# Last value tile of a masked attention read-out: its third piece sent as two transfers, rows 0 to 119 and rows 120 to 127

## The chip, the cores and the metric

One core of a Trainium2 chip runs the whole kernel. The metric is the device time of one execution in microseconds; smaller is better. Everything is float32.

## What is computed

For 512 users, each with 200 items of 64 numbers, the reference forms a query, scores the items, masks them, takes the softmax, and sums the projected values:

```python
B, L, D = (512, 200, 64)
scaler = jnp.float32(D) ** 0.5
q = target_key @ W_target.T
k = jnp.einsum('bld,ed->ble', item_keys, W_item)
v = jnp.einsum('bld,ed->ble', item_values, W_value)
scores = jnp.einsum('bd,bld->bl', q, k) / scaler
scores = scores + -100000000.0 * (1.0 - mask.astype(scores.dtype))
w = jax.nn.softmax(scores, axis=1)
return jnp.einsum('bl,bld->bd', w, v)
```

## The kernel before, in words

Keys and values are 26 MB each, and nearly all of the time is spent bringing them in. The kernel never projects keys or values: the query goes through both weight matrices first, and the value weights are applied once to the weighted sum.

The users go in four blocks (`NBLK`) of 128. Each block has two key tiles and two value tiles (`NT`), each of 128 rows by 6400 numbers, which is 3200 KB. `key_ring` and `value_ring` have two slots each, `s` = 0 and 1. SyncE (SP) issues all of these transfers from one queue, in the order key 0, key 1, value 0, value 1, and from the second block on it waits with each issue until TensorE (PE) has used up the slot (`s_key_used`, `s_value_used`).

A value tile has three regions along its row: 2 "eighth" column groups of 128 numbers, 16 "half" groups, and 32 "full" groups. TensorE works them off in `weigh(n, s)`: `weigh_full(s, k)` for k = 0 to 7 issues four matmuls each (L378), and `weigh_rest(s)` issues 2 for the eighths (L387) and 16 for the halves (L393). For slot 0 the full groups come first and the rest after; for slot 1 it is the other way round. All of them add up in `ps_context`. A float32 matmul stands in the trace as two records, so the 32 full matmuls of a tile are 64 records.

The very last value tile (block 3, slot 1) is not one transfer but four, cut along the row at `CUTS = (0, 5, 7, PAIRS_T)` (L162):

- piece 0: eighths and halves, 2304 numbers of each row, 1152 KB
- piece 1: the full groups of k = 0 to 4, 2560 numbers, 1280 KB
- piece 2: the full groups of k = 5 and 6, 1024 numbers, 512 KB
- piece 3: the full groups of k = 7, 512 numbers, 256 KB

Each has its own semaphore `s_value_piece[c]`, and TensorE waits for it before `weigh_rest`, before k = 0, before k = 5 and before k = 7. After the last matmul a short tail follows: VectorE copies the context (L306), TensorE transposes it (L422), VectorE masks it (L314), TensorE projects it (L430), ScalarE scales it (L233) and sends it out (L236).

Of the kernel before, what the change touches and what calls it, by code (L numbers as in the profile page):

```python
# [10 lines left out]
P = 128  # L11
# [21 lines left out]
def masked_attention_kernel(nc, w_query, targets, w_value_cols, mask_rows, keys, values, out):  # L33
# [13 lines left out]
    HALF_AT = EIGHTHS_T * VB  # L47
    FULL_AT = HALF_AT + N_HALF * VB
    CUTS = (0, 5, 7, PAIRS_T)

    out_blocks = out.rearrange("(n u) d -> n u d", u=P)

    with ExitStack() as ctx:
        def sb(name, shape, dt=F32):
            return ctx.enter_context(nc.sbuf_tensor(name, shape, dt))
# [4 lines left out]
        def sem(name):  # L60
            return ctx.enter_context(nc.semaphore(name))

        key_ring = sb("key_ring", [P, NT, KCOLS])
        value_ring = sb("value_ring", [P, NT, VCOLS])
# [46 lines left out]
        s_value = [sem(f"s_value{s}") for s in range(NT)]  # L111
        s_value_piece = [sem(f"s_value_piece{c}") for c in range(len(CUTS))]
        s_key_used = sem("s_key_used")
# [33 lines left out]
        @block.sync  # L147
        def _(sp):
            for n in range(NBLK):
                for s in range(NT):  # L150
                    if n > 0:
                        sp.wait_ge(s_key_used, NT * (n - 1) + s + 1)
                    sp.dma_start(key_ring[:, s, :], keys[n * NT + s]).then_inc(s_key[s], 16)
                for s in range(NT):
                    if n > 0:
                        sp.wait_ge(s_value_used, NT * (n - 1) + s + 1)
                    tile = values[n * NT + s]
                    if n == NBLK - 1 and s == NT - 1:
                        begin = 0
                        for c, cut in enumerate(CUTS):  # L160
                            end = FULL_AT + cut * GRP * VB
                            sp.dma_start(value_ring[:, s, begin:end], tile[:, begin:end]) \  # L162
                                .then_inc(s_value_piece[c], 16)
                            begin = end
                    else:
                        sp.dma_start(value_ring[:, s, :], tile).then_inc(s_value[s], 16)
# [166 lines left out]
        def _(pe):  # L333
# [41 lines left out]
            def weigh_full(s, k):  # L375
                for g in range(GRP):
                    c = FULL_AT + (k * GRP + g) * VB
                    last = nc.tensor.matmul(  # L378
                        ps_context[g * GU:(g + 1) * GU, 0:VB], window(sta_full, PITCH, g, s * PAIRS_T + k),
                        value_ring[:, s, c:c + VB], start=s == 0 and k == 0,  # L380
                        stop=s == NT - 1 and k == PAIRS_T - 1)
                return last

            def weigh_rest(s):
                for k in range(EIGHTHS_T):
                    g = s * EIGHTHS_T + k
                    nc.tensor.matmul(ps_context[g * GU:(g + 1) * GU, 0:VB],  # L387
                                     sta_eighth[:, g].rearrange("p i e -> p (i e)"),
                                     value_ring[:, s, k * VB:(k + 1) * VB], start=False, stop=False)
                for k in range(HALVES_T):  # L390
                    for g in range(GRP):
                        c = HALF_AT + (k * GRP + g) * VB
                        last = nc.tensor.matmul(  # L393
                            ps_context[g * GU:(g + 1) * GU, 0:VB], window(sta_half, PITCH_H, g, s * HALVES_T + k),
                            value_ring[:, s, c:c + VB], start=False, stop=False)
                return last

            def weigh(n, s):
                in_pieces = n == NBLK - 1 and s == NT - 1
                if not in_pieces:  # L400
                    pe.wait_ge(s_value[s], 16 * (n + 1))
                if s == 0:
                    pe.wait_ge(s_sta_full, n + 1)
                    if n > 0:
                        pe.wait_ge(s_context, n)
                    for k in range(PAIRS_T):
                        weigh_full(s, k)
                    pe.wait_ge(s_sta_rest, 3 * (n + 1))
                    last = weigh_rest(s)
                else:  # L410
                    if in_pieces:
                        pe.wait_ge(s_value_piece[0], 16)
                    weigh_rest(s)
                    for k in range(PAIRS_T):
                        if in_pieces and k in CUTS:
                            pe.wait_ge(s_value_piece[CUTS.index(k) + 1], 16)
                        last = weigh_full(s, k)
                last.then_inc(s_value_used, 1)

# [12 lines left out]
            for n in range(NBLK):  # L432
                for s in range(NT):
                    score(n, s)
                    if n == 0 and s == 0:
                        nc.tensor.matmul(ps_query[:, P:B], w_both[:], targets_sb[:, P:B], start=True, stop=True) \  # L436
                            .then_inc(s_query, 1)
                    if n > 0 and s == 0:
                        turn_context(n - 1)
                    if n > 0 and s == NT - 1:  # L440
                        project(n - 1)
                turn_weights(n)
                for s in range(NT):
                    weigh(n, s)
# [42 lines left out]
```

## Time and profile before

| | us |
|---|---|
| median of 3 runs | 136.64 (136.59 to 137.13) |
| the profiled execution, its own time | 137.14 |
| its span, first to last instruction | 135.3 |
| outside the span | 1.8 |
| TensorE busy | 76.6 (57%) |
| data moved | 53.34 MB, 394 GB/s on average |

The profile gives times in microseconds from the start of the span. In its table of 40 slices each digit is a busy share in tenths. "Granted clock" (PEclk) is 1.00 where TensorE runs at 2.4 GHz and 0.50 where it runs at 1.2 GHz. The DMA share is the mean over the 16 DMA engines of the core, so that a single busy engine shows as about 0.06.

### The profile page before, as it was taken

The page shows a single profiled execution, that of the slowest core. Times are in us where ns is not written, and L with a number is a line of the kernel's source. Part 1 is how long each engine was busy: PE and PEld are TensorE (multiplying, and loading weights), DVE is VectorE, ACT ScalarE, POOL GpSimd, SP SyncE. Part 2 cuts the span into 40 slices and gives each one's busy share as a digit, 9 for nine tenths or more (in the row PEclk, how much of TensorE's full clock was granted, in tenths as well). Part 3 has the DMA queues.
Part 4 walks back from the last instruction along what each step waited for, and adds up shares of the span by engine and source line. Part 5 has one row for each costly group of instructions (what it writes and reads, how often), then busy time and mean ns, then how long its engine had stood idle before and what let it go on. Part 6 is the DMA issues. An engine that isn't in the chain of part 4 may idle for free.

```text
span 135.3 us, 2879 instructions
## 1 busy us (share of the span) xinstructions
PE 76.6 (57%) x1342; PEld 54.4 (40%) x1342; DVE 12.9 (10%) x46; ACT 7.3 (5%) x22; POOL 5.6 (4%) x15
## 2 busy tenths in 40 slices
PE   0002299839180592949362393949462393957981
PEld 0000164529180351528261261628362251626970
DVE  5000000340000000022000000022000000022000
ACT  0300000030000000030000000030000000030000
POOL 7500000010000000010000000010000000010000
PEclk9999999986999559595999559595999559595599
DMA  5999999999999998999999999999999999999710
GB/s 144 428 392 376 400 423 421 456 383 462 413 439 431 416 459 386 462 401 456 396 449 444 401 462 391 446 431 434 419 426 446 398 462 409 439 387 412 322 36 10
DMA packets 3771, 53.34 MB, mean 394 GB/s; under 512 B 1072, under 2 KB 1136, under 8 KB 1584
## 3 DMA queue, kind: packets, MB, share of 16 engines
q1 hardware_dynamic: 2736, 52.43, 91.8%
q10 hardware_dynamic: 1024, 0.74, 1.7%
q8 instruction: 10, 0.16, 0.5%
q14 instruction: 1, 0.01, 0.0%
HBM read 53.04 MB, written 0.13 MB: 393 GB/s over the span
## 4 chain that ended last, share of the span: by engine, by line
DMA 69%; PE 25%; issue 1%; ACT 1%; ACTq 1%; DVE 1%; POOL 0%; DVEq 0%
DMA key_ring<-keys 39%; DMA value_ring<-values 20%; PE ps_scores L356 13%; DMA targets_sb<-targets 11%; PE ps_context L378 6%; PE ps_context L393 3%; PE ps_query L436 1%; PE ps_small L430 1%; PE ps_query L340 1%; ACT result L233 0%; PE ps_context L387 0%; ACT expd L220 0%; ACTq L196 0%; PE ps_turn_rest L370 0%; POOL half_twice L191 0%
## 5 line engine op out<-in xcount | busy, mean ns | idle before, releaser
L356 PE MATMUL ps_scores<-key_ring,sta_query 128*32 128x200 f32 x512 | 37.5, 473 | 21.7 <-DMA key_ring<-keys 21.2
L356 PEld LDWEIGHTS ps_scores<-key_ring,sta_query 128*32 128x32 f32 x512 | 22.2, 155 | 35.8 <-DMA key_ring<-keys 22.6
L378 PE MATMUL ps_context<-value_ring,sta_full 128*32 128x128 f32 x512 | 21.9, 337 | 2.1 <-DMA value_ring<-values 2.1
L378 PEld LDWEIGHTS ps_context<-value_ring,sta_full 128*32 128x32 f32 x512 | 19.1, 139 | 4.2 <-DMA value_ring<-values 3.4
L393 PE MATMUL ps_context<-value_ring,sta_half 128*32 128x128 f32 x256 | 10.8, 294 | 0.0
L387 PE MATMUL ps_context<-value_ring,sta_eighth 128*32 128x128 f32 x32 | 3.7, 314 | 9.9 <-DMA value_ring<-values 9.9
L393 PEld LDWEIGHTS ps_context<-value_ring,sta_half 128*32 128x32 f32 x256 | 8.7, 118 | 0.2
L335 PE MATMUL ps_small<-w_query_sb 64*64 64x128 f32 x2 | 0.7, 444 | 10.9 <-DMA w_query_sb<-w_query 10.9
L233 ACT ACTIVATE result<-ps_small,inv_sum 128x64 f32<-128x64 f32 x4 | 1.3, 314 | 97.1 <-PE ps_small L430 97.1
L191 POOL COPY half_twice<-expd 128x128 f32<-128x128 f32 x4 | 1.4, 351 | 114.8 <-ACT expd L220 114.8
L387 PEld LDWEIGHTS ps_context<-value_ring,sta_eighth 128*32 128x32 f32 x32 | 1.8, 126 | 10.7 <-DMA value_ring<-values 10.7
L306 DVE COPY context<-ps_context 128x128 f32<-128x128 f32 x4 | 1.2, 292 | 38.7 <-PE ps_context L378 38.7
L366 PE MATMUL ps_turn_full<-ident,expd 128*128 128x128 f32 x4 | 1.3, 322 | 6.1 <-ACT expd L220 6.1
L335 PEld LDWEIGHTS ps_small<-w_query_sb 64*64 64x64 f32 x2 | 0.3, 200 | 10.9 <-DMA w_query_sb<-w_query 10.9
L314 DVE TENSOR_TENSOR context_t<-ps_small,own_parity 128x128 f32<-128x128 f32 x4 | 1.2, 292 | 30.0 <-PE ps_small L422 30.0
L272 DVE TENSOR_TENSOR biased<-ps_scores,mask_bias 128x200 f32<-128x200 f32 x4 | 1.5, 367 | 21.5 <-PE ps_scores L356 21.5
L366 PEld LDWEIGHTS ps_turn_full<-ident,expd 128*128 128x128 f32 x4 | 0.6, 139 | 6.9 <-ACT expd L220 5.0
L340 PE MATMUL ps_query<-targets_sb,w_both 64*128 64x128 f32 x2 | 0.8, 482 | 4.2 <-DMA targets_sb<-targets 4.2
L220 ACT ACTIVATE expd<-biased,neg_max 128x200 f32<-128x200 f32 x4 | 1.8, 462 | 12.0 <-DVE neg_max L275 12.0
L340 PEld LDWEIGHTS ps_query<-targets_sb,w_both 64*128 64x128 f32 x2 | 0.5, 306 | 4.6 <-issue 4.6
L264 DVE COPY sta_query<-ps_query 64x64 f32<-64x64 f32 x4 | 1.0, 256 | 13.1 <-PE ps_query L340 13.1
L430 PE MATMUL ps_small<-w_value_twice,context_t 128*128 128x64 f32 x8 | 1.7, 295 | 0.5 <-DVE context_t L314 0.5
(35 smaller groups left out, 26.7 us busy)
## 6 DMA issues: line engine op xcount, KB each, us to landing
key_ring<-keys SPq DMA_DIRECT2D x8, 3200.0 KB, 25.5
value_ring<-values SPq DMA_DIRECT2D x7, 3200.0 KB, 27.4
value_ring<-values SPq DMA_DIRECT2D x1, 1280.0 KB, 26.0
value_ring<-values SPq DMA_DIRECT2D x1, 1152.0 KB, 23.3
value_ring<-values SPq DMA_DIRECT2D x1, 512.0 KB, 26.8
mask_sb<-mask_rows ACTq DMA_DIRECT2D x1, 400.0 KB, 22.3
value_ring<-values SPq DMA_DIRECT2D x1, 256.0 KB, 26.9
targets_sb<-targets ACTq DMA_DIRECT2D x1, 128.0 KB, 14.3
```

The source lines that it names most:

```text
L191: nc.gpsimd.tensor_copy(half_twice[:], expd[:, FULL:FULL + HALF].unsqueeze(1).to_broadcast([P, 2, HALF])) \
L220: nc.scalar.activation(expd[:], biased[:], ACT.Exp, bias=neg_max[:, 0:1], scale=1.0, accum_out=exp_sum[:, n:n + 1]).then_inc(s_exp, 1)
L233: nc.scalar.activation(result[:, n, :], ps_project, ACT.Copy, scale=inv_sum[:, n:n + 1]) \
L272: nc.vector.tensor_tensor(biased[:], ps_scores[:, 0:L], mask_bias[:, n, :], ALU.add) \
L340: nc.tensor.matmul(ps_query[:, 0:P], w_both[:], targets_sb[:, 0:P], start=True, stop=True) \
L356: last = nc.tensor.matmul(ps_scores[g * GU:(g + 1) * GU, 0:L], window(sta_query, PITCH, g, s * PAIRS_T + k), key_ring[:, s, c:c + KB], sta ...
L366: nc.tensor.transpose(ps_full_t, expd[:, 0:FULL], ident[:]).then_inc(s_turn_full, 1)
L378: last = nc.tensor.matmul(ps_context[g * GU:(g + 1) * GU, 0:VB], window(sta_full, PITCH, g, s * PAIRS_T + k), value_ring[:, s, c:c + VB], ...
L387: nc.tensor.matmul(ps_context[g * GU:(g + 1) * GU, 0:VB], sta_eighth[:, g].rearrange("p i e -> p (i e)"), value_ring[:, s, k * VB:(k + 1) ...
L393: last = nc.tensor.matmul(ps_context[g * GU:(g + 1) * GU, 0:VB], window(sta_half, PITCH_H, g, s * HALVES_T + k), value_ring[:, s, c:c + VB ...
L430: nc.tensor.matmul(ps_project, context_t[:], w_value_twice[:], start=True, stop=True).then_inc(s_project, 1)
L436: nc.tensor.matmul(ps_query[:, P:B], w_both[:], targets_sb[:, P:B], start=True, stop=True) \
```

## The change

Piece 2 becomes two transfers with the same columns: one of rows 0 to 119 and one of rows 120 to 127. Both count on the same semaphore, and TensorE waits for 32 in place of 16 there. The other pieces stay whole. The matmuls, their order and their operands are the same.

```diff
     CUTS = (0, 5, 7, PAIRS_T)
+
+    ROW_PARTS = ((slice(0, P),), (slice(0, P),), (slice(0, 120), slice(120, P)), (slice(0, P),))
...
                             end = FULL_AT + cut * GRP * VB
-                            sp.dma_start(value_ring[:, s, begin:end], tile[:, begin:end]) \
-                                .then_inc(s_value_piece[c], 16)
+                            for rows in ROW_PARTS[c]:
+                                sp.dma_start(value_ring[rows, s, begin:end], tile[rows, begin:end]) \
+                                    .then_inc(s_value_piece[c], 16)
                             begin = end
...
                     if in_pieces:
-                        pe.wait_ge(s_value_piece[0], 16)
+                        pe.wait_ge(s_value_piece[0], 16 * len(ROW_PARTS[0]))
                     weigh_rest(s)
                     for k in range(PAIRS_T):
                         if in_pieces and k in CUTS:
-                            pe.wait_ge(s_value_piece[CUTS.index(k) + 1], 16)
+                            c = CUTS.index(k) + 1
+                            pe.wait_ge(s_value_piece[c], 16 * len(ROW_PARTS[c]))
                         last = weigh_full(s, k)
```

This is the end of SyncE's queue before. Each row is one transfer, with its shape in rows by numbers of 4 bytes; the first two rows are the last key tiles and the value tile for slot 0.

```order
L153 DMA key_ring<-keys 128x6400 [waits s_key_used] x2
L166 DMA value_ring<-values 128x6400 [waits s_value_used]
L162 DMA value_ring<-values 128x2304 [waits s_value_used]
L162 DMA value_ring<-values 128x2560
L162 DMA value_ring<-values 128x1024
L162 DMA value_ring<-values 128x512
```

And the same place in the changed kernel.

```order
L155 DMA key_ring<-keys 128x6400 [waits s_key_used] x2
L169 DMA value_ring<-values 128x6400 [waits s_value_used]
L165 DMA value_ring<-values 128x2304 [waits s_value_used]
L165 DMA value_ring<-values 128x2560
L165 DMA value_ring<-values 120x1024
L165 DMA value_ring<-values 8x1024
L165 DMA value_ring<-values 128x512
```

One transfer of 128x1024 has become one of 120x1024 and one of 8x1024, both ahead of the last piece and with no new wait; nothing else has moved.

## Rows read from the trace of the kernel before

**Rows 1.** The page's 40 slices: TensorE, its clock, the DMA engines.

```profile
PE   0002299839180592949362393949462393957981
...
PEclk9999999986999559595999559595999559595599
DMA  5999999999999998999999999999999999999710
GB/s 144 428 392 376 400 423 421 456 383 462 413 439 431 416 459 386 462 401 456 396 449 444 401 462 391 446 431 434 419 426 446 398 462 409 439 387 412 322 36 10
```

**Rows 2.** Chain of work that ended last, its end: start, length, what.

```profile
96.19 26.72 DMA value_ring<-values
122.91 0.04 issue
122.95 3.64 PE ps_context L378 x64
...
129.64 1.80 PE ps_context L378 x64
131.44 0.02 issue
131.46 0.30 DVE context L306
...
133.13 0.31 ACT result L233
```

**Rows 3.** The four issues of L162: first and last start, time to landing.

```profile
L162 SPq DMA_DIRECT2D value_ring<-values x4: 327/432/438, 102.5 to 103.8; - x4
...
DMA to landing us min/median/max: 23.3/26.4/26.9
```

**Rows 4.** DMA issues: count, KB each, time from issue to landing.

```profile
value_ring<-values SPq DMA_DIRECT2D x1, 1280.0 KB, 26.0
value_ring<-values SPq DMA_DIRECT2D x1, 1152.0 KB, 23.3
value_ring<-values SPq DMA_DIRECT2D x1, 512.0 KB, 26.8
...
value_ring<-values SPq DMA_DIRECT2D x1, 256.0 KB, 26.9
```

**Rows 5.** SyncE's timeline: piece 1 alone, then pieces 2 and 3 merged.

```profile
102.87 0.44 SPq L162 DMA_DIRECT2D value_ring<-values  x1
103.35 0.91 SPq L162 DMA_DIRECT2D value_ring<-values  x2
```

**Rows 6.** Windows, with PE busy, PEld, DVE, ACT, POOL, PEclk, DMA share, GB/s.

```profile
117.00:118.00 1.00, 1.00 (x20) 0.64 (x16) 0.00 (x0) 0.00 (x0) 0.00 (x0) 0.50 1.01 435
126.50:127.00 0.50, 0.50 (x16) 0.45 (x14) 0.00 (x0) 0.00 (x0) 0.00 (x0) 0.50 1.02 411
127.60:128.00 0.40, 0.40 (x16) 0.35 (x12) 0.00 (x0) 0.00 (x0) 0.00 (x0) 0.50 0.54 215
128.00:128.40 0.40, 0.40 (x16) 0.37 (x12) 0.00 (x0) 0.00 (x0) 0.00 (x0) 0.50 0.52 210
128.80:129.20 0.40, 0.40 (x24) 0.40 (x20) 0.00 (x0) 0.00 (x0) 0.00 (x0) 1.00 0.39 128
129.20:129.60 0.40, 0.40 (x25) 0.40 (x20) 0.00 (x0) 0.00 (x0) 0.00 (x0) 1.00 0.17 66
129.75:129.95 0.20, 0.20 (x16) 0.20 (x12) 0.00 (x0) 0.00 (x0) 0.00 (x0) 1.00 0.08 31
130.15:130.30 0.15, 0.15 (x16) 0.15 (x8) 0.00 (x0) 0.00 (x0) 0.00 (x0) 1.00 0.07 27
130.30:130.70 0.40, 0.40 (x24) 0.40 (x20) 0.00 (x0) 0.00 (x0) 0.00 (x0) 1.00 0.00 0
```

**Rows 7.** Timeline of TensorE: the full groups of slot 0, then of slot 1.

```profile
122.95 3.64 PE L378 MATMUL ps_context<-value_ring,sta_full 128*32 128x128 f32 x64 [0.94 <-DMA value_ring<-values]
129.47 1.92 PE L378 MATMUL ps_context<-value_ring,sta_full 128*32 128x128 f32 x64
```

## The prediction

> **What bounds the kernel now.** I read the 40 slices first. The DMA engines are at nine tenths or more from the second slice to the 37th, at 353 to 462 GB/s, with TensorE busy in bursts between waits: for most of its length this kernel is a stream of 53 MB, and no edit behind that stream is worth more than its last few microseconds [rows 1]. So I went to the end of the chain of waits. It says that the value tile of slot 0 lands at 122.91 us, that TensorE then works without a gap until 131.44 us (3.64 us for the full groups of slot 0, the last full groups for 1.80 us at the end), and that a tail of small steps follows, from the copy at 131.46 us to the scaling at 133.13 us [rows 2]. The question for this change is whether piece 2 or piece 3 of the last tile is late for TensorE.
>
> When the four pieces land: the issues run from 102.5 us to 103.8 us, and the landings are 23.3, 26.0, 26.8 and 26.9 us behind them [rows 3, 4]. Piece 0 lands at 102.5 + 23.3 = 125.8 us. Piece 1 is issued at 102.87 us and lands at 128.9 us; piece 2 is issued at 103.35 us and lands at 130.1(5) us; piece 3 lands at 103.8 + 26.9 = 130.7 us [rows 3 to 5].
>
> When TensorE wants them: the full groups of slot 1 begin at 129.47 us and take 1.92 us for 64 records [rows 7]. A record lasts about 0.27 us and four column groups overlap, so the eight steps start (1.92 - 0.39) / 7 = 0.22 us apart, where 0.39 us is what the last step needs to its end (its second pass starts 0.11 us after the first and then lasts 0.27 us). Step k = 0 starts at 129.47, k = 5 at 130.56 and k = 7 at 131.0 us. The slack is therefore 0.6 us for piece 1, 0.4 us for piece 2 and 0.3 us for piece 3. TensorE waits for none of them. The 64 records need 1.92 us at the high clock, and the busy time in the windows from 128.80 to 130.70 us is the whole window each time [rows 6], so no short wait is hidden there.
>
> Why TensorE is the last to finish is the clock: the granted clock is 0.50 (1.2 GHz) in the windows from 126.50 to 128.40 us and 1.00 (2.4 GHz) from 128.80 us on [rows 6]. The full groups cost 3.64 us at the low clock for slot 0, and 1.92 us at the high one for slot 1 [rows 7].
>
> The data side has a feature of its own. Until 127 us all engines run (share 1.02, 411 GB/s), then they drop out one after another: 0.54 at 127.60 us, 0.39 at 128.80 us, 0.17 at 129.20 us. From 129.75 us to about 130.3 us the windows show 31 and 27 GB/s, and then nothing [rows 6]. A full load of 435 GB/s over 16 engines is 27 GB/s for each [rows 6], so that last half microsecond is **one engine alone**. Its last bytes pass by about 130.3 us and the landing is counted at 130.7 us, 0.4 us later.
>
> **The change part by part.**
>
> 1. One more transfer on SyncE's queue, ahead of piece 3. Its own issue costs at most 0.45 us (the issue of piece 1 takes 0.44 us, and two take 0.91 us [rows 5]). Nothing is queued behind it but piece 3, which is then issued at about 104.3 us, against data that flows after 126 us. The 20-odd us of data already in the queue hide this. If the cover were gone, piece 3 would be 0.45 us later. Cost: 0.
>
> 2. Rows 120 to 127 are moved apart from the rest. The trace doesn't show which engine carries which row, so I bound this. The bytes are the same, and on an even spread each engine has 8 rows of 4 KB of piece 2, 32 KB, which at 27 GB/s is 1.2 us; one row is 0.15 us. From below: if the engine that is alone at the end is the one that loses its rows, it is done with piece 3 1.2 us sooner, and the next engines set the landing. Those stop between 129.60 and 129.75 us (66 GB/s in the window to 129.60 us, one engine's rate from 129.75 us [rows 6]), with 0.4 us to the landing and up to one row more: piece 3 at 130.0 to 130.2 us in place of 130.7 us. From above: if that engine instead gets a ninth row, piece 3 lands at 130.7 + 0.15 = 130.85 us, which is still ahead of 131.0 us. In both cases the matmuls of k = 7 start when they do now. Cost: 0, between -0.3 and +0.95 us by the rivals below.
>
> 3. TensorE's wait ahead of k = 5 is for 32 and no longer 16. It is the same instruction. Behind it on TensorE are the 12 matmuls of k = 5 to 7 and with them the tail. It is met when both parts have landed: 130.15 us or earlier, 130.3 us with a ninth row on the last engine, and k = 5 starts at 130.56 us. Cost: 0.
>
> The sum on the profiled execution is 137.14 + 0 = 137.1 us. It is made of a span of 135.3 us and 1.8 us around it, and the change touches only the span. That execution is 0.5 us above the median and equal to the highest run (137.13), so for the median I carry the zero over: **136.6 us**.
>
> A rule that speaks against the change is in the Trainium skill, DMA: Bandwidth & Descriptors, "Rules for kernel authors": two transfers to disjoint halves of the partitions aren't worth it, since both go over all 16 engines. By that rule the split gives nothing and costs an issue, which is the same sum as mine.
>
> **The rivals.**
>
> *The last engine is relieved, and it counts.* In the profiled execution the low clock makes TensorE late. Suppose that in other executions the clock rises earlier; the same tiles in the rows at 2.4 GHz need 1.92 us in place of 3.64 us, so TensorE would catch up with the data before 128.9 us. Then k = 0 starts at 128.9 us with piece 1, k = 5 would be due at 130.0 us and waits for piece 2 until 130.15 us, k = 7 would be due at 130.6 us and waits for piece 3 until 130.7 us, and the last step ends at 131.1 us. With the last engine relieved, pieces 2 and 3 are no longer late, piece 1 is the only one that counts, and the end is 128.9 + 1.9 = 130.8 us. The gain is 0.3 us: 136.3 us. It can't be more, since piece 1 is not split and the last engine carries it as before. For it speaks that two of the three runs shown are 0.5 us shorter than the profiled execution; against it, that the profile shows a slack on every piece, and that nothing in it says that the last engine is the one with rows 120 to 127. The condition is a clock that rises at least 0.3 us earlier in the last tile.
>
> The Trainium skill has a rule for this rival in DMA: Bandwidth & Descriptors, "Why a DMA increments its semaphore by 16 and not by 1": the number of engines is the largest up to 16 that divides the slowest dimension, so 120 rows go on 15 engines and 8 rows on 8, the lowest-numbered ones. The same page calls engines 7 and 15 usually slower, with a doubtful cause. No row here shows the split by engines; if both hold, the engine that is alone at the end could be the sixteenth, and the gain is what this rival has, 0.3 us at most.
>
> *Nothing is relieved.* The engine that is late is not the one that loses rows, or the 120 rows fall on the engines in another way than eight each. The landings stay within 0.15 us, and the time is 136.6 us, as forecast.
>
> *Slower: the eight rows fall on one engine.* If the small transfer isn't spread and goes on one engine on top of its eight rows of the other part, that engine has 1.2 us more to do. If it is among the late ones, piece 2 lands at 131.3 us and piece 3 at up to 130.7 + 1.2 = 131.9 us. TensorE then waits at k = 5 (due 130.56 us) and at k = 7, which starts at about 131.95 us in place of 131.0 us: +0.95 us, 137.6 us. It decides from the point at which piece 3 is over 0.3 us later. An engine that is done 1.2 us ahead of the last would absorb it all. For it speaks only that 8 rows are few; against it, that most engines are done before 129.2 us (share 0.39 falling to 0.17 [rows 6]), so an arbitrary engine has room for it.
>
> **How the numbers follow.** No wait on the path moves: 0.50, at 136.6 us. Nothing is relieved: 0.16, also 136.6 us. The relief counts: 0.27, at 136.3 us. The eight rows on one late engine: 0.07, at up to 137.6 us. The forecast is 136.6 us. The range takes in the relief with the spread of the runs below the median (136.3 - 0.1 = 136.2 us), and above it the highest run (137.13 us), rounded to 137.15 us; the slower rival's upper half is left out, as are stray runs. A measurement of this kernel tells 0.5%, 0.68 us, from no change. The relief is at most 0.3 us and stays within that, save for executions that differ more than I can see, so faster gets 0.04. Slower gets 0.05, the part of that rival above 0.68 us and a little for strays. The same gets 0.91.
>
> **What would show it.** In the profile of the changed kernel the issues of the last tile should be five, with piece 3 issued 0.4 to 0.5 us later than before. Step 2 is seen in the DMA windows after 129.2 us: if the last engine is relieved, the stretch at 27 to 31 GB/s is gone and piece 3 lands at about 130.1 us after an unchanged slot 0 landing at 122.9 us; if not, it stays. The chain should still run from the value tile of slot 0 through TensorE without a wait to its last full group at 131.4 us. I am wrong if the chain shows a DMA of the last tile as the last to be waited for, if piece 3 lands after 131.0 us, or if TensorE's clock in the last tile is not what it was; the last would say nothing on the change, since no matmul ahead of k = 5 is touched by it.

## The result: 1.85% slower

| | before | changed |
|---|---|---|
| median of 6 runs, us | 136.67 (136.47 to 137.13) | 139.06 (138.66 to 140.6) |
| the profiled execution, its own time | 137.14 | 139.99 |
| its span | 135.3 | 138.2 |

The ratio of the changed kernel to the kernel before is 1.0185 (95% interval 1.0154 to 1.0216), and the medians differ by 2.4 us. The forecast was no change, in a range up to 137.15 us, and it missed. The profiled execution of the changed kernel is 0.9 us above its median.

The chain of waits of the changed kernel, at its end (start, length, what), answers to [rows 2]:

```profile
104.16 26.61 DMA value_ring<-values
130.76 0.04 issue
130.81 3.55 PE ps_context L381 x64
134.36 0.02 issue
134.38 0.30 DVE context L309
```

Its last wait is no longer for the value tile of slot 0 but for a piece of the last tile. The issue at 104.16 us is of this piece, and the sizes tell which one it is (KB each, time to landing, as in [rows 4]):

```profile
104.16 0.44 SPq L165 DMA_DIRECT2D value_ring<-values  x1
...
value_ring<-values SPq DMA_DIRECT2D x1, 1280.0 KB, 26.6
```

It is **piece 1**, the one in front of the piece that was split, and the change doesn't touch it. TensorE's timeline shows what that does (it answers to [rows 7]):

```profile
122.58 1.96 PE L381 MATMUL ps_context<-value_ring,sta_full 128*32 128x128 f32 x64 [1.33 <-DMA value_ring<-values]
...
125.62 1.14 PE L396 MATMUL ps_context<-value_ring,sta_half 128*32 128x128 f32 x30
130.81 3.50 PE L381 MATMUL ps_context<-value_ring,sta_full 128*32 128x128 f32 x64 [4.05 <-DMA value_ring<-values]
```

Slot 0 landed 0.4 us earlier than before (122.5 against 122.9 us), TensorE ran at its high clock through both tiles' first parts and was out of work before 127 us. Then it waited 4.05 us. Piece 1 landed at 130.76 us instead of 128.9 us. Piece 3 was issued last, at 105.5 us, and landed at 105.5 + 27.7 = 133.2 us instead of 130.7 us:

```profile
L165 SPq DMA_DIRECT2D value_ring<-values x5: 288/438/835, 103.8 to 105.5; - x5
...
value_ring<-values SPq DMA_DIRECT2D x1, 256.0 KB, 27.7
```

The last tile was also issued 1.3 us later here (103.8 against 102.5 us), but that is not what makes piece 1 late. Piece 0, issued 1.3 us later as well, landed at 103.8 + 21.6 = 125.4 us, ahead of its 125.8 us before. Two of the runs below say the same: one with piece 1 issued at 103.99 us has it at 128.6 us, one with piece 1 issued at 102.36 us has it at 131.0 us.

The windows (PE, PEld, DVE, ACT, POOL, PEclk, DMA share, GB/s) say what the DMA engines did meanwhile, first of the changed kernel:

```profile
126.00:127.00 1.00, 0.76 (x25) 0.49 (x16) 0.00 (x0) 0.00 (x0) 0.00 (x0) 1.00 1.02 230
127.00:128.00 1.00, 0.00 (x0) 0.00 (x0) 0.00 (x0) 0.00 (x0) 0.00 (x0) 1.00 0.87 209
```

The same first microsecond of the kernel before:

```profile
126.00:127.00 1.00, 1.00 (x24) 0.90 (x20) 0.00 (x0) 0.00 (x0) 0.00 (x0) 0.50 1.00 408
```

The DMA share is 1.02 and the rate is 230 GB/s: all engines are busy, at little more than half of their rate. In the kernel before a busy share of 1.00 goes with 408 GB/s. That pair of numbers is the finding of this profile.

The packed trace tells more than its views print: how long each packet took. A packet is one row of one transfer, so its size names its piece: 10240 bytes in piece 1, 4096 in piece 2, 2048 in piece 3. These are the mean times of a packet, in ns; for piece 1 only packets count that started after the first packet of piece 2, at about 124.9 us:

| run | piece 1 | piece 2 | piece 3 |
|---|---|---|---|
| before | 385 | 159 | 84 |
| changed | 576 | 248 | 126 |
| piece 2 by columns (below) | 385 | 84 (half as wide) | 84 |
| rows 0 to 119 of piece 2 alone (below) | 560 | 233 | 129 |
| piece 2 whole, eight rows extra (below) | 406 | 164 | 91 |

Ahead of piece 2 a packet of piece 1 takes 394 ns in the changed kernel and 395 ns in the kernel before. So the packets of pieces that the change leaves alone are slowed as well, once those of piece 2 flow beside them. The trace also has the moment at which each of the sixteen engines reports on a transfer's semaphore that its share has landed (its "completion"). The completions of piece 1 show the same. The first is there at 125.3 us in both kernels and the sixth at 125.9 and 126.0 us; but the ninth comes at 128.0 us in the changed kernel and at 127.1 us before, and the sixteenth at 130.8 and 128.8 us. The question for the experiments is why engines that move no more bytes take twice as long for them.

### The profile page after: what moved, and what is told of

Read it like the earlier page. It is cut to its first block, busy times and chain, and to the rows that moved or that the text cites. A ratio compares the mean times of both kernels' runs of the same rounds, so it can differ in the third digit from the quotient of the medians.

```text
span 138.2 us, 2880 instructions
## 1 busy us (share of the span) xinstructions
PE 79.7 (58%) x1342; PEld 58.8 (43%) x1342; DVE 12.9 (9%) x46; ACT 7.2 (5%) x22; POOL 5.6 (4%) x15
## 4 chain that ended last, share of the span: by engine, by line
DMA 82%; PE 13%; SPq 1%; issue 1%; DVE 0%; ACT 0%; DVEq 0%
DMA value_ring<-values 82%; PE ps_context L381 9%; PE ps_context L396 3%; PE ps_context L390 1%; SPq L155 1%; SPq L169 0%; PE ps_small L434 0%; PE ps_small L426 0%; SPq L165 0%; ACT result L236 0%; DVE context_t L317 0%; DVE context L309 0%; DVEq L316 0%
## 5 line engine op out<-in xcount | busy, mean ns | idle before, releaser
L359 PE MATMUL ps_scores<-key_ring,sta_query 128*32 128x200 f32 x512 | 34.3, 441 | 17.6 <-DMA key_ring<-keys 17.1
L359 PEld LDWEIGHTS ps_scores<-key_ring,sta_query 128*32 128x32 f32 x512 | 20.6, 144 | 30.0 <-DMA key_ring<-keys 18.5
L381 PE MATMUL ps_context<-value_ring,sta_full 128*32 128x128 f32 x512 | 26.1, 378 | 8.9 <-DMA value_ring<-values 8.9
L381 PEld LDWEIGHTS ps_context<-value_ring,sta_full 128*32 128x32 f32 x512 | 23.1, 156 | 10.8 <-DMA value_ring<-values 9.9
L396 PE MATMUL ps_context<-value_ring,sta_half 128*32 128x128 f32 x256 | 14.1, 347 | 0.0
L396 PEld LDWEIGHTS ps_context<-value_ring,sta_half 128*32 128x32 f32 x256 | 10.9, 135 | 0.4
L223 ACT ACTIVATE expd<-biased,neg_max 128x200 f32<-128x200 f32 x4 | 1.8, 461 | 11.5 <-DVE neg_max L278 10.9
L434 PEld LDWEIGHTS ps_small<-w_value_twice,context_t 128*128 128x128 f32 x8 | 1.4, 216 | 2.0 <-issue 2.0
## 6 DMA issues: line engine op xcount, KB each, us to landing
value_ring<-values SPq DMA_DIRECT2D x7, 3200.0 KB, 25.6
value_ring<-values SPq DMA_DIRECT2D x1, 1152.0 KB, 21.6
value_ring<-values SPq DMA_DIRECT2D x1, 256.0 KB, 27.7
targets_sb<-targets ACTq DMA_DIRECT2D x1, 128.0 KB, 14.0
```

What stands on the lines that cost most here:

```text
L223: nc.scalar.activation(expd[:], biased[:], ACT.Exp, bias=neg_max[:, 0:1], scale=1.0, accum_out=exp_sum[:, n:n + 1]).then_inc(s_exp, 1)
L359: last = nc.tensor.matmul(ps_scores[g * GU:(g + 1) * GU, 0:L], window(sta_query, PITCH, g, s * PAIRS_T + k), key_ring[:, s, c:c + KB], sta ...
L381: last = nc.tensor.matmul(ps_context[g * GU:(g + 1) * GU, 0:VB], window(sta_full, PITCH, g, s * PAIRS_T + k), value_ring[:, s, c:c + VB], ...
L396: last = nc.tensor.matmul(ps_context[g * GU:(g + 1) * GU, 0:VB], window(sta_half, PITCH_H, g, s * HALVES_T + k), value_ring[:, s, c:c + VB ...
L434: nc.tensor.matmul(ps_project, context_t[:], w_value_twice[:], start=True, stop=True).then_inc(s_project, 1)
```

## The experiments

**The theories.** A: the 120-row transfer gives its rows to the engines in another pattern than a 128-row transfer, so that several engines write through the same path (a "port") into the on-chip memory at once. B: one transfer more costs an issue and a completion. C: the 8-row transfer does the harm. D: what counts is how many engines take part. The clock is a fifth suspect, as a follow-on.

**One transfer more, but all rows in each (B).** Piece 2 cut by columns:

```diff
+                            halves = 2 if c == 2 else 1
+                            step = (end - begin) // halves
+                            for h in range(halves):
+                                at = begin + h * step
+                                sp.dma_start(value_ring[:, s, at:at + step], tile[:, at:at + step]) \
+                                    .then_inc(s_value_piece[c], 16)
```

> Piece 2 is cut into two transfers by columns (512 numbers each, k = 5 and k = 6), both of all 128 rows, TensorE waits for 32 as in the changed kernel. It keeps everything of the change but the rows: one more issue on the queue, one more completion, a wait for 32. 
Measured: 136.78 us against 136.88 us, ratio 0.9979 (0.995 to 1.0009). Its chain ends with piece 1, issued late and landing early:

```profile
103.99 24.65 DMA value_ring<-values
128.64 0.04 issue
128.69 2.38 PE ps_context L382 x64
```

B falls: a fifth transfer, a second completion and a wait for 32 cost nothing that shows. The difference lies in the rows.

**The 120-row part alone (A against C).**

```diff
-    ROW_PARTS = (..., (slice(0, 120), slice(120, P)), ...)
+    ROW_PARTS = (..., (slice(0, 120),), ...)
```

> Only rows 0 to 119 of piece 2 are sent; rows 120 to 127 of it are left out, so the weighted sums of k = 5 and 6 use what the previous tile left in those rows. Theory A (the 120-row transfer and its pattern of rows): most of the loss is here, 138.0 to 139.2 us, and in the windows the DMA share stays near 1 while the rate is about half of 430 GB/s once piece 2 flows. Theory C, the 8-row transfer: eight engines write the same eight rows' part of the memory and hold up the rest; without it the time is back at 136.4 to 136.9 us.

Measured: 138.94 us against 136.88 us, ratio 1.0163 (1.0086 to 1.024), though it moves 32 KB less. Its windows show the same pair of numbers:

```profile
126.00:127.00 1.00, 1.00 (x24) 0.92 (x18) 0.00 (x0) 0.00 (x0) 0.00 (x0) 0.50 1.03 236
```

And its chain ends with piece 1 again, as the size tells:

```profile
102.36 28.63 DMA value_ring<-values
131.00 0.04 issue
131.04 2.13 PE ps_context L381 x64
...
value_ring<-values SPq DMA_DIRECT2D x1, 1280.0 KB, 28.6
```

By the medians 2.1 us of the 2.4 us are in the 120-row transfer.

**The 8-row part alone (C).** Piece 2 whole, and an extra copy of its rows 120 to 127 behind it into a spare tile:

```diff
+                            if c == 2:
+                                sp.dma_start(spare[120:P, :], tile[120:P, begin:end]).then_inc(s_spare, 16)
```

> Piece 2 goes whole (128 rows) as before, and behind it an extra transfer copies rows 120 to 127 of it into rows 120 to 127 of a spare tile that nothing reads; 32 KB more than before. Theory C (the 8-row transfer does the harm): 138 to 139.2 us. Theory A: eight engines have one row of 4 KB more, all on two write paths, so up to 4 x 0.15 = 0.6 us on these paths, but behind piece 2 only: 136.6 to 137.4 us.

Measured: 136.97 us against 136.88 us, ratio 1.0015 (0.998 to 1.005). C falls as the cause of the 2.4 us; a cost of some tenths is not excluded.

**All 16 engines in both parts (D).** `(slice(0, 112), slice(112, P))`.

> Piece 2 is split into rows 0 to 111 and 112 to 127. Both numbers can be divided by 16, so all 16 engines can take part in each (7 rows and 1 row). Theory D, fewer engines: the loss comes from the 120 rows being on 15 engines and the 8 rows on 8; here it is gone, 136.7 us. Theory A: with 7 rows in a row for each engine, the pattern differs from that of 128 rows as much as with 120, and the loss stays in large part: 137.5 to 139.2 us.

Measured: 138.93 us against 136.88 us, ratio 1.0156 (1.0082 to 1.0229). Piece 2's semaphore gets 32 completions from the DMA engines here, and 23 in the changed kernel (15 and 8), so the split by 112 and 16 rows does use all engines twice. D, in the form that leaving one engine out is what costs, falls: 112 and 16 rows are as bad as 120 and 8.

**The transfers measured by themselves.** The most telling run has no kernel in the way. Nine transfers of the first value tile are put ahead of the work, each waited for (one execution):

```diff
+            def alone(n):
+                sp.wait_ge(s_alone, 16 * n)
+            sp.dma_start(value_ring[0:128, 0, :], values[0][0:128, :]).then_inc(s_alone, 16)
+            alone(1)
+            sp.dma_start(value_ring[0:120, 0, :], values[0][0:120, :]).then_inc(s_alone, 16)
+            alone(2)
...
```

> Ahead of the work of before, nine transfers of the first value tile, 25.6 KB for each row, each issued when the one before has landed, so that nothing else flows beside them but the four small loads at the start: rows 0-127, 0-119, 0-111, 0-95, 0-63, 32-95, 64-127, 120-127, 0-7. At 430 GB/s 128 rows are 7.6 us, one row on one engine 0.95 us, plus about 2 us for issue and landing. Theory A, shared write paths, with the port map of the Trainium skill, SBUF: State Buffer, section Door 1 (four rows share a port, rows 32 apart share it too, rows 0 to 63 use eight ports and rows 64 to 127 the other eight): rows 32-95 take 3.8 + 2 us, rows 0-63 and 64-127 7.6 + 2 us though they are as many bytes; rows 0-119 take more than 128 rows, up to 15.2 + 2 us; 8 rows on two ports take 3.8 + 2 us. Theory D (only the number of engines counts): 0-63, 32-95 and 64-127 all take 3.8 + 2 us, 0-119 as long as 0-127 (8 rows on each engine), and 8 rows 0.95 + 2 us. The whole is longer than before by the sum of the nine.

SyncE's timeline (start, length of the issue) is all that is needed, since each issue follows the landing of the one before. The lines are, in order, rows 0-127, 0-119, 0-111, 0-95, 0-63, 32-95, 64-127, 120-127, 0-7, and the first real issue:

```profile
0.81 0.37 SPq L152 DMA_DIRECT2D value_ring<-values  x1
12.65 0.41 SPq L154 DMA_DIRECT2D value_ring<-values  x1
30.32 0.32 SPq L156 DMA_DIRECT2D value_ring<-values  x1
44.30 0.31 SPq L158 DMA_DIRECT2D value_ring<-values  x1
57.34 0.54 SPq L160 DMA_DIRECT2D value_ring<-values  x1
68.15 0.54 SPq L162 DMA_DIRECT2D value_ring<-values  x1
75.22 0.49 SPq L164 DMA_DIRECT2D value_ring<-values  x1
85.68 0.28 SPq L166 DMA_DIRECT2D value_ring<-values  x1
90.93 0.28 SPq L168 DMA_DIRECT2D value_ring<-values  x1
96.04 0.83 SPq L174 DMA_DIRECT2D key_ring<-keys  x2
```

| rows | issue to next issue, us | mean time of a packet (one row), us |
|---|---|---|
| 0-127 (beside the small loads of the start) | 11.8 | 1.05 |
| 0-119 | 17.7 | 1.90 |
| 0-111 | 14.0 | 1.54 |
| 0-95 | 13.0 | 1.80 |
| 0-63 | 10.8 | 1.89 |
| 32-95 | 7.1 | 1.15 |
| 64-127 | 10.5 | 1.91 |
| 120-127 | 5.3 | 2.43 |
| 0-7 | 5.1 | 2.37 |

The last column is from the packets of the packed trace; the fastest of them took 0.95 us. Rows 0-63 and rows 32-95 are the same number of rows and bytes, with 16 completions from the engines in both, and take 10.8 and 7.1 us. And 120 rows take 5.8 us longer than 128. Two windows of this run, inside rows 0-127 and inside rows 0-119, repeat the pair of numbers:

```profile
3.00:10.00 7.00, 0.00 (x0) 0.00 (x0) 0.53 (x5) 1.28 (x1) 2.20 (x2) 1.00 0.97 411
15.00:29.00 14.00, 0.00 (x0) 0.00 (x0) 0.00 (x0) 0.00 (x0) 0.00 (x0) 1.00 0.89 192
```

A has the order of the times right, but not their size: its 2 us for issue and landing are too few, since rows 32-95 took 7.1 us for 5.8, rows 0-63 and 64-127 10.8 and 10.5 us for 9.6, and rows 0-119 17.7 us for at most 17.2. Only the eight rows came in below A's value, at 5.3 and 5.1 us for 5.8, and still 2.2 to 2.3 us above the 2.95 us that D had. A wanted four engines on one path to take four times as long for a row; the packets took 2.4 us, two and a half times the 0.95 us. Why it isn't four is open.

The measured 10.8, 7.1, 10.5 and 17.7 us fit this, and so do packets of 1.9 us in place of 0.95 us. Which engine gets which rows of a 120-row transfer no run shows: the 8 rows in a row for each are A's assumption.

**Where it is written or where it is read, and what it does to the transfer ahead.** Again alone, in one execution:

> Again transfers alone, ahead of the work of before, each group waited for (25.6 KB a row; in the measurement before, rows 0-63 took 10.8 us from issue to next issue, rows 32-95 7.1 us, of which about 3 us are issue, start and landing; 128 rows at full rate are 7.6 + 3 us). (1) 128 rows; (2) rows 0-63 of the tile filled from rows 32-95 of the source; (3) rows 32-95 of the tile filled from rows 0-63 of the source: if the limit lies where the rows are written, (2) takes 10.8 and (3) 7.1 us; if it lies where they are read, the other way round. (4) rows 32-91 (60 rows, 15 engines with 4 rows each, no shared write path): 7.1 us. (5) two whole tiles, issued together: 15.2 + 3 us. (6) a whole tile and rows 0-119 of a second: if a 120-row transfer only slows itself, 7.6 + 17.7 = 25 us; if it also crosses the tile ahead of it, the same sum or more, and the rate falls before the first tile is through. (7) the same with rows 120-127 behind: 2 to 3 us more than (6).

```profile
12.58 0.54 SPq L154 DMA_DIRECT2D value_ring<-values  x1
23.00 0.54 SPq L156 DMA_DIRECT2D value_ring<-values  x1
29.53 0.41 SPq L158 DMA_DIRECT2D value_ring<-values  x1
36.16 0.36 SPq L160 DMA_DIRECT2D value_ring<-values  x1
36.56 0.43 SPq L161 DMA_DIRECT2D value_ring<-values  x1
53.93 0.33 SPq L163 DMA_DIRECT2D value_ring<-values  x1
54.30 0.44 SPq L164 DMA_DIRECT2D value_ring<-values  x1
79.68 0.33 SPq L166 DMA_DIRECT2D value_ring<-values  x1
...
108.47 0.83 SPq L174 DMA_DIRECT2D key_ring<-keys  x2
```

Rows 0-63 written from rows 32-95 of the source took 10.4 us (L154), rows 32-95 written from rows 0-63 took 6.5 us (L156): the limit is on the writing side. Rows 32-91, 60 rows, took 6.6 us (L158), with 15 completions from the engines: leaving one engine out is harmless as such. Two whole tiles took 17.8 us (L160 and L161), a tile and 120 rows 25.8 us (L163, L164), and the same with the last 8 rows behind 28.8 us (from L166 to the first real issue). So a tile sent as 120 + 8 rows costs 11.0 us more than a whole one of 3200 KB. Piece 2 has 512 KB: 11.0 x 512 / 3200 = **1.8 us**, an estimate to lay beside the 2.4 us measured.

In the pair the rate falls only when the first tile is nearly through (windows within the pair of tile and 120 rows):

```profile
56.00:63.00 7.00, 0.00 (x0) 0.00 (x0) 0.00 (x0) 0.00 (x0) 0.00 (x0) 1.00 0.99 421
64.00:77.00 13.00, 0.00 (x0) 0.00 (x0) 0.00 (x0) 0.00 (x0) 0.00 (x0) 1.00 0.97 207
```

There the engines run nearly abreast: the sixteen completions of the first of two whole tiles lie 0.7 us apart. Even so the tile ahead suffers a little; its last engine reports 10.2 us after the issue with a whole tile behind, and 11.5 and 11.2 us with 120 rows behind. In the kernel the engines are further apart. The completions for one piece lie 3.5 us apart (125.3 to 128.8 us for piece 1, before), so at 126 us the ones ahead are in piece 2 while the ones behind have piece 1 left.

**Which splits are bad, in the kernel.** Rows 0-63 and 64-127; rows 32-95, 0-31 and 96-127; and the split by 120 and 8 on piece 3 instead of piece 2:

> Piece 2 as rows 0 to 63 and rows 64 to 127, 4 rows on each of 16 engines in both. Measured alone, a 64-row transfer of either half took as long as its rows would on eight engines. Theory A (write paths shared by rows; each half reaches only half of them): as slow as the changed kernel, 138.3 to 139.3 us. Rival (what matters is that 120 or 112 rows leave uneven numbers on the engines): even numbers here, 136.9 us.

> Piece 2 as three transfers: rows 32 to 95 (256 KB, 4 rows on each engine; measured alone, this one ran at full rate), rows 0 to 31 and rows 96 to 127 (2 rows on each engine, each on half of the write paths). One transfer more than rows 64 + 64. Theory A: half of the bytes flow freely and the rest crosses, so about half of the loss or less: 136.9 to 138.0 us. Rival (splitting by rows costs, whatever the rows): as slow as the changed kernel or slower, 139 us.

> The same split by 120 and 8 rows, but of piece 3 (256 KB) and not of piece 2 (512 KB). Theory A: half the bytes go in the bad pattern and fewer engines are still writing pieces 0 and 1 then: half of the loss or less, 137.2 to 138.0 us. Rival (a fixed cost of such a split, whatever its size): 139 us.

| piece and rows | median, us | ratio | 95% interval |
|---|---|---|---|
| 2: 0-63, 64-127 | 139.39 | 1.0169 | 1.0133 to 1.0204 |
| 2: 32-95, 0-31, 96-127 | 138.6 | 1.0113 | 1.0064 to 1.0162 |
| 3: 0-119, 120-127 | 137.83 | 1.005 | 1.0026 to 1.0074 |

The kernel before had 137.11 us beside these three. Even numbers of rows don't help (first line); half of the bytes in a harmless pattern, with even one transfer more, takes away some two fifths of the loss, less than expected (138.0 at most); half of the bytes on the last piece is less than a third of the loss. The packets of piece 1 say the same, measured as in the table above: 610 ns with rows 0-63 and 64-127, 439 ns with three parts, 404 ns with the split on piece 3, against 385 ns. The profile of the split on piece 3 shows both waits, for piece 1 and for piece 2 before k = 5; it is of the slowest of ten executions, 1.1 us above the median:

```profile
129.51 1.30 PE L381 MATMUL ps_context<-value_ring,sta_full 128*32 128x128 f32 x40 [2.43 <-DMA value_ring<-values]
131.33 1.51 PE L381 MATMUL ps_context<-value_ring,sta_full 128*32 128x128 f32 x24 [0.52 <-DMA value_ring<-values]
```

**The share of the clock.** In the changed kernel's profile the last full groups took 3.50 us and not 1.92, at 1.2 GHz after the long wait (granted clock 0.50 from 131 us). How much of the time is the clock's can be bounded: piece 3 landed at 133.2 us, and the last step takes 0.4 us, so at the high clock the last full group would have ended at 133.6 us at the earliest, against 134.36 us. That is at most 0.8 us.

The runs above answer it too. In three of their profiled executions the last full groups ran at a granted clock of 1.00, and the loss was there: 138.79 us (rows 0 to 119 alone), 138.48 us (112 and 16 rows) and 139.39 us (64 and 64 rows), which is 1.6 to 2.3 us above the medians of before. The last of them:

```profile
131.52 2.20 PE L381 MATMUL ps_context<-value_ring,sta_full 128*32 128x128 f32 x64 [2.78 <-DMA value_ring<-values]
```

The changed kernel with TensorE kept at work in that wait, by matmuls of the identity into an unused part of `ps_query`:

```diff
                     weigh_rest(s)
+                    if in_pieces:
+                        keep_busy(14)
```

> The changed kernel with 14 extra matmuls of the identity with itself, into a part of ps_query that is no longer read, between weigh_rest of the last tile and the wait for piece 1; about 3 us at 2.4 GHz, in the stretch where TensorE otherwise waits. They change no transfer. If a part of the loss is the clock that falls to 1.2 GHz in that wait (the profiled execution took 3.5 us for the last full groups, 1.9 at the high clock), the slow executions of 139.2 to 140.6 us go and the median is 138.3 to 138.8 us; if the clock has no share in the median, it stays at 139.0 us. It can't come back to 136.7 us, since the landing of piece 1 is late by itself.

Measured: 139.69 us against 137.11 us, ratio 1.0197 (1.0161 to 1.0234): no gain that shows. The profile of this run, at 139.35 us, has the last full groups at the high clock:

```profile
128.21 3.39 PE L403 MATMUL ps_query<-ident 128*128 128x128 f32 x28
131.53 1.95 PE L381 MATMUL ps_context<-value_ring,sta_full 128*32 128x128 f32 x64
```

The loss is there without the low clock. The run is not clean on the size, since the extra matmuls end 0.8 us after piece 1 landed. Piece 1 was issued at 103.64 us and took 27.1 us, so it landed at 130.7 us:

```profile
103.64 0.44 SPq L165 DMA_DIRECT2D value_ring<-values  x1
...
value_ring<-values SPq DMA_DIRECT2D x1, 1280.0 KB, 27.1
```

Piece 3 landed at 105.0 + 27.7 = 132.7 us there, and TensorE's last full group ended at 133.5 us, so at most 0.4 us of gain are hidden. What the low clock adds to the changed kernel's median isn't settled beyond these bounds.

The same on the kernel before, with 6 and 4 extra matmuls in the last block's two waits:

> The kernel before with extra matmuls of the identity with itself on TensorE in the last block: 6 where it waits for the last softmax and 4 where it waits for the value tile of slot 0, so that its clock is up when the last tiles come. This is the condition of my rival 'the last engine is relieved, and it counts', without the change of the transfers. If the low clock in the last tile costs anything in the median, 136.3 to 136.5 us where before has 136.7; if most executions end by the last landing of the data anyway, the median stays within 0.15 us and only the upper executions (137.1 and up) may go.

Measured: 137.13 us against 136.84 us, ratio 1.0024 (0.9999 to 1.0049). Nothing is gained, and the upper executions didn't go; the median rose by 0.3 us where at most 0.15 us were expected. Its profile, with the clock up, waits for the data instead, and the last full group ends at 131.44 us, where it ended before:

```profile
128.75 1.30 PE L378 MATMUL ps_context<-value_ring,sta_full 128*32 128x128 f32 x40 [1.26 <-DMA value_ring<-values]
130.53 0.91 PE L378 MATMUL ps_context<-value_ring,sta_full 128*32 128x128 f32 x24 [0.48 <-DMA value_ring<-values]
```

**Which engine is late.** Three small transfers behind piece 3, and one clear on GpSimd behind each:

```diff
+                        for c, rows in enumerate((slice(0, 8), slice(32, 92), slice(0, P))):
+                            sp.dma_start(spare[rows, c, :], tile[rows, 0:128]).then_inc(s_probe[c], 16)
```

> The kernel before, with three small transfers behind piece 3 (512 bytes a row, into a spare tile): rows 0-7, rows 32-91, rows 0-127. GpSimd waits for each in this order and clears one column of another spare tile after each wait, so that the three clears show when they landed. By the Trainium skill (DMA: Bandwidth & Descriptors, section on why a DMA increments its semaphore by 16) they use the 8, 15 and 16 lowest-numbered engines. If the engine that is alone at the end is the sixteenth, the clear behind rows 0-127 comes 0.5 to 0.8 us behind the other two; if it is among the first eight, all three come together; if it is one of the ninth to fifteenth, the first comes ahead of the second and the third follows at once. Measured alone, none of this changes the time of the kernel by more than 0.3 us.

```profile
129.64 0.10 POOL L200 MEMSET seen<- 128x1 f32 x1 [10.38 <-DMA spare<-values]
130.80 0.26 POOL L200 MEMSET seen<- 128x1 f32 x2 [1.06 <-DMA spare<-values]
```

The 8-row transfer landed at 129.6 us, and the 60-row and the 128-row one nearly together, at 130.8 and 130.9 us. So the late engine is one that 60 rows use and 8 rows don't. By the rule on the number of engines in the Trainium skill, DMA: Bandwidth & Descriptors, section "Why a DMA increments its semaphore by 16 and not by 1", it is one of the ninth to fifteenth, and the engine that 120 rows leave out isn't it. On how many engines take part the trace agrees, with 8, 15 and 16 completions for the three; it doesn't say which engines they are. This is one execution.

## Why the prediction was wrong

- **What bounds the kernel.** Right for the profiled execution, and too narrow for the others. The slack of 0.3 to 0.6 us on the pieces came from a low clock in that execution; with the clock up, TensorE waits for pieces 1 and 2 (the run with extra matmuls on the kernel before). The prediction had this as a condition of its first rival. The end is set by the landings to within a few tenths either way, so anything that slows them has little slack to eat through. (The 353 GB/s that the prediction reads from the slices isn't there: the lowest of slices 2 to 37 is 376, and one of them has its engines at eight tenths. Nothing hangs on it.)
- **Step 1, one more issue: 0.** Right; the split by columns measured it (0.9979, at most 1.0009).
- **Step 2, rows 120 to 127 moved apart: this is the step that failed.** It was bounded by where the eight rows go, at 0.15 us a row and 27 GB/s an engine. It took the price of a row as fixed and asked only how many rows an engine has. The term that was missing is what becomes of the other 120: written in another pattern, they go at half rate (192 GB/s alone against 411; 230 and 209 GB/s in the kernel against 408). A row of piece 2 took 0.25 us in place of 0.16 us, and the rows of pieces 1 and 3 beside it took half as long again. Step 2 gave piece 3 a landing between 130.0 and 130.85 us; it landed at 133.2 us. The cost is 1.8 us by the estimate from the transfers alone and 2.4 us measured, and 2.1 us of it remain when the eight rows aren't sent at all.
- **The victim.** The sum looked for the cost at piece 2 and piece 3. It came first at piece 1, which the change leaves alone: +1.9 us on its landing, 128.9 to 130.76 us. Pieces 2 and 3 are later too, at 132.8 and 133.2 us against 130.1 and 130.7 us; with TensorE at its high clock they would be its last waits. The dropping-out of engines one after another had been read in the windows [rows 6], but only as room for an idle engine, not as time in which engines ahead and engines behind write different pieces.
- **Step 3, the wait for 32: 0.** Right as a cost of its own.
- **The rule cited.** The rule of the Trainium skill (DMA: Bandwidth & Descriptors, "Rules for kernel authors") that two parts of the rows aren't worth it was taken to mean no gain and no loss; here two halves cost 1.7%. The port map of the Trainium skill (SBUF — State Buffer, "Door 1: The DMA port swizzle") was not weighed. By itself it would not have given the loss, since rows 0 to 119 reach all sixteen ports; it also takes a guess at which rows each engine has.
- **The rivals.** The slower one had the right side and the wrong mechanism: the eight rows weren't on one engine (eight engines report for them), and an 8-row transfer by itself cost nothing measurable (1.0015). The relief had no engine to relieve in the one execution that tells, where the late engine isn't the sixteenth, and the half rate would have buried its 0.3 us anyway. The slow engines 7 and 15 that were brought up for it are no support either: the Trainium skill (DMA: Bandwidth & Descriptors, "Latency and other measured facts") puts them down to transfers issued from GpSimd, and here SyncE and ScalarE issue them all.
- **What the profile should have shown.** Five issues: yes. "I am wrong if the chain shows a DMA of the last tile as the last to be waited for": it does. "If piece 3 lands after 131.0 us": it landed at 133.2 us.

In the profiled executions the account closes: the full groups of slot 1 start 1.34 us later (130.81 against 129.47 us) and take 1.58 us longer (3.50 against 1.92 us), 2.9 us together, and the spans differ by 138.2 - 135.3 = 2.9 us. Of these 2.9 us at most 0.8 us are the clock's, since piece 3 landed only at 133.2 us; the median differs by 2.4 us.

No version here beats the kernel before. A harmless way to spare one engine needs rows that keep to the pattern, such as 32 to 91, and the rows outside of these then cross: the three-part split that was closest to it lost 1.1%.

## What to carry to other kernels

A transfer's rows are part of its cost. Before a tile is split by rows, ask which engines write which rows at once; splitting by columns keeps the pattern and was free here. And where a window shows the DMA engines fully busy at half the rate, look for a conflict between them, not for missing work. Here every piece in flight beside the crossing one paid, the one that was not edited first.

## What was not expected of the hardware

- Rows 0-63 and rows 32-95 of the same width, on an idle queue: 10.8 and 7.1 us; the difference follows the rows written, not the rows read (10.4 and 6.5 us with the sources exchanged).
- 120 rows took 17.7 us and 128 rows at most 11.8 us: fewer bytes, 5.8 us more.
- A transfer in a crossing pattern slows the packets of whole transfers beside it: 576 ns in place of 385 ns for a row of 10240 bytes of piece 1.
- Eight neighbouring rows of 25.6 KB alone took 5.1 to 5.3 us from issue to next issue, three quarters of the 7.1 us of 64 rows in the good pattern; each row took 2.4 us in place of 0.95 us.
- The 16 engines are 3.5 us apart at the end of the kernel, and in one execution the late one was among those that a 60-row transfer uses and an 8-row one doesn't.
